# Local attention in a fused kernel: P times V on four tiles behind the scores, and two engines' order within a slot

## The reference, cut to the local attention

```python
def local_attention(q, k, v):                 # b, h, n, d = 8, 16, 256, 64
    nw = n // w                               # w = 32
    bk2, bv2 = (look(bk), look(bv))           # the previous window and the own one
    mask = (it < jb) | (it > jb + w) | (jb == -1)
    sim = jnp.einsum('bhwie,bhwje->bhwij', bq, bk2) * QK_SCALE
    sim = jnp.where(mask, -jnp.finfo(sim.dtype).max, sim)
    attn = jax.nn.softmax(sim, -1)
    out = jnp.einsum('bhwij,bhwje->bhwie', attn, bv2)

def attn_layer(x, Wqkv, qs, ksc, Wo):
    ...
    q = l2norm(q) * qs
    k = l2norm(k) * ksc
    ...
    q = q * cos * scale + rotate_half(q) * sin * scale
    k = k * cos * inv + rotate_half(k) * sin * inv
    out = local_attention(q, k, v)
    return out.transpose(0, 2, 1, 3).reshape(b, n, INNER) @ Wo
```

## Time and profile before

| | kernel before |
|---|---|
| median of three runs | 2608.39 us (2608.14 to 2609.6) |
| profiled execution | 2614.84 us |
| its span, first to last instruction | 2613.1 us |
| TensorE matmul, busy | 2374.6 us (91%) |
| VectorE, busy | 1954.8 us (75%) |
| ScalarE, busy | 1797.4 us (69%) |
| GpSimd, busy | 1083.0 us (41%) |
| mean granted TensorE clock | 0.971 of full speed |

### The profile page before, as it was taken

How to read it: one execution, slowest core, us unless ns; L and a number is a source line. 1 busy time by engine, 2 the same in 40 slices (tenths; PEclk the granted TensorE clock), 3 DMA queues, 4 the chain that set the end, 5 groups by cost and what they waited for, 6 DMA issues and landing times. The chain is left out here.

```text
span 2613.1 us, 62460 instructions
## 1 busy us (share of the span) xinstructions
PE 2374.6 (91%) x24940; PEld 1232.9 (47%) x24940; DVE 1954.8 (75%) x2595; ACT 1797.4 (69%) x2593; POOL 1083.0 (41%) x461
## 2 busy tenths in 40 slices
PE   7799999999999999999999999999999887777778
PEld 3355555455554555545545555454555432222345
DVE  5678777788777887787778787787777668999442
ACT  4677777787677776777767777677777566545533
POOL 0354444444444444444444444444444204556030
PEclk8899999999999999999999999999999988989889
DMA  0100000000000000000000000000000010000001
GB/s 21 54 2 2 2 26 10 10 2 2 15 22 11 2 2 15 22 11 2 2 14 14 19 2 2 15 14 19 2 2 2 1 37 1 0 0 0 18 25 40
DMA packets 16047, 29.92 MB, mean 11 GB/s; under 512 B 3616, under 2 KB 6064, under 8 KB 15664
## 3 DMA queue, kind: packets, MB, share of 16 engines
q1 hardware_dynamic: 15760, 25.78, 3.2%
HBM read 24.73 MB, written 1.05 MB: 10 GB/s over the span
## 5 line engine op out<-in xcount | busy, mean ns | idle before, releaser
L709 POOL TENSOR_TENSOR f_rot<-f_raw,f_tabc 128x1024 f32<-128x1024 f32 x192 | 452.9, 2359 | 682.6 <-DVE f_qk L757 299.3
L713 POOL TENSOR_TENSOR f_rot<-f_rot,f_shuf 128x1024 f32<-128x1024 f32 x192 | 453.6, 2362 | 465.1 <-DVE f_shuf L750 465.1
L607 ACT ACTIVATE f_raw<-f_ps 128x1024 f32<-128x1024 f32 x192 | 196.7, 1024 | 303.4 <-PE f_ps L431 301.6
L478 PEld LDWEIGHTS f_ps<-f_ptz,f_v 64*64 64x64 f32 x6144 | 260.1, 133 | 93.9 <-issue 93.9
L478 PE MATMUL f_ps<-f_ptz,f_v 64*64 64x96 f32 (+1 forms) x6144 | 286.4, 243 | 1.5 <-ACT f_ptz L628 1.4
L776 DVE TENSOR_REDUCE f_sum<-f_ps 128x8 f32<-128x512 f32 x192 | 131.9, 687 | 178.9 <-ACT f_ps L663 176.1
L747 DVE STREAM_SHUFFLE f_shuf<-f_raw 128x1024 f32<-128x1024 f32 x192 | 255.7, 1332 | 0.0
L757 DVE SCALAR_TENSOR_TENSOR f_qk<-f_rn,f_rot 128x1024 f32<-128x1024 f32 x192 | 233.7, 1217 | 28.9 <-POOL f_rot L713 28.9
L430 PE MATMUL f_ps<-f_xs,f_wq 128*128 128x512 f32 x384 | 216.1, 645 | 34.3 <-DVE f_xs L728 24.2
L750 DVE TENSOR_TENSOR f_shuf<-f_shuf,f_tabs 128x1024 f32<-128x1024 f32 x192 | 236.8, 1233 | 7.6
L616 ACT ACTIVATE f_rn<-f_ps 128x1024 f32<-128x1024 f32 x192 | 199.0, 1036 | 38.9 <-PE f_ps L437 38.6
(11 more groups left out here) (267 smaller groups left out, 4010.0 us busy)
## 6 DMA issues: line engine op xcount, KB each, us to landing
e_w<-in_e_w SPq DMA_DIRECT2D x16, 256.0 KB, 2.8
f_wq<-in_f_wq SPq DMA_DIRECT2D x12, 256.0 KB, 2.9
f_wk<-in_f_wk SPq DMA_DIRECT2D x12, 256.0 KB, 3.6
f_wv<-in_f_wv SPq DMA_DIRECT2D x12, 256.0 KB, 3.3
f_wo<-in_f_wo SPq DMA_DIRECT2D x6, 512.0 KB, 3.2
f_w<-in_f_w SPq DMA_DIRECT2D x6, 341.0 KB, 2.9
s_dx<-in_k_pick SPq DMA_DIRECT2D x1, 1536.0 KB, 9.4
f_w<-in_f_w SPq DMA_DIRECT2D x6, 192.0 KB, 3.4
```

The lines of the kernel that those rows point to most:

```text
L478: mm = pe.matmul(view(ps, 7 * CH + 64 * p, [1, n], p0=64 * h, rows=64), v[64 * h:64 * h + 64, p * CH + 64 * j:p * CH + 64 * j + 64], ptz[6 ...
L709: pool.tensor_tensor(view(rot, 0, [S, 4], [1, S]), view(raw, 0, [S, 4], [1, S]), view(tab_c, 0, [S, 2], [0, 2], [1, S]), ALU.mult).then_in ...
L713: pool.tensor_tensor(rot[:, :], rot[:, :], shuf[:, :], ALU.add).then_inc(sem["rot"], 1)
```

## The change

It has four parts.

- Values are laid out anew: partitions 0 to 63 hold tokens of the first sequence and 64 to 127 those of the second, for all heads, where before they held the two heads of each pair. Two matmuls of 512 columns on two tiles take the place of four of 256.
- P times V: `mix` runs its 16 matmuls of 64 rows by 64 columns on all four quarters of the array (rows by sequence, columns by head) and writes banks 6 and 7, one for each sequence. Before, they ran on two quarters and wrote bank 7. Scores, mask, exponential, `s` and the output copy are laid out to match. Since bank 6 is also that of the transposes, `turn` now waits for the output copy.
- The order on TensorE and ScalarE: `mix` stands behind the scores and ahead of the projections in every slot; the output copy stands ahead of the raw copy and the squares.
- The order on VectorE: `rotate` stands ahead of `soft_b`.

ScalarE's squares stood ahead of the exponential before as well.

```diff
--- before.py
+++ after.py
@@ -412,12 +412,10 @@
                     need(pe, sem["ln2"], i)
                 if q == 0:
                     need(pe, sem["gelu"], i * 3 - 6 + 1 + G0)
-                for r in range(2):
-                    for h in range(2):
-                        at = 128 * (q % 4) + 64 * r
-                        mm = pe.matmul(view(ps, 2 * CH + 256 * r, [1, 256], p0=64 * h, rows=64), xs[:, at:at + 64],
-                                       view(wv, CH * (q // 4) + 64 * h, [128, 4], [1, 64]),
-                                       start=(r == 0), stop=True, skip_group_check=True)
+                for b in range(2):
+                    at = S * b + 64 * (q % 4)
+                    mm = pe.matmul(view(ps, 2 * CH, [1, CH], p0=64 * b, rows=64), xs[:, at:at + 64],
+                                   wv[:, CH * (q // 4):CH * (q // 4) + CH], start=True, stop=True)
                 mm.then_inc(sem["v_mm"], 1)
 
             def project(i, j):
@@ -454,7 +452,8 @@
 
                         keys = (view(t, KOFF + WIN * w, [-WIN, 2], [1, WIN], p0=64 * h, rows=64) if w % 2 == 0
                                 else view(t, KOFF + WIN * (w - 1), [1, 2 * WIN], p0=64 * h, rows=64))
-                        mm = pe.matmul(view(ps, (4 + h) * CH + (w // 4) * 64, [1, 64], p0=WIN * (w % 4), rows=WIN),
+                        four, b = w // 4 % 2, w // 8
+                        mm = pe.matmul(view(ps, (4 + h) * CH + (2 * four + b) * 64, [1, 64], p0=WIN * (w % 4), rows=WIN),
                                        t[64 * h:64 * h + 64, WIN * w:WIN * w + WIN], keys, start=False, stop=True,
                                        skip_group_check=True)
                 mm.then_inc(sem["s_mm"], 1)
@@ -462,6 +461,7 @@
             def turn(i, j):
                 need(pe, sem["p"], i * 8 + j + 1)
                 need(pe, sem["ptz"], i * 8 + j)
+                need(pe, sem["o"], i * 8 + j)
                 for t in range(4):
                     mm = pe.transpose(view(ps, 6 * CH + 128 * t, [1, 128]), s[j % 2][:, 128 * t:128 * t + 128], ident[:, :])
                 mm.then_inc(sem["t_mm"], 1)
@@ -472,13 +472,14 @@
                 gather(sem["o"], i * 8 + j)
                 if j % 4 == 0:
                     gather(sem["v"], i * 8 + j + 4)
-                for p in range(8):
-                    n = 96 if p < 7 else 64
+                for p in range(4):
+                    n = 96 if p < 3 else 64
                     for h in range(2):
-                        mm = pe.matmul(view(ps, 7 * CH + 64 * p, [1, n], p0=64 * h, rows=64),
-                                       v[64 * h:64 * h + 64, p * CH + 64 * j:p * CH + 64 * j + 64],
-                                       ptz[64 * h:64 * h + 64, 96 * p:96 * p + n],
-                                       start=(p == 0), stop=(p == 7), skip_group_check=True)
+                        for b in range(2):
+                            mm = pe.matmul(view(ps, (6 + b) * CH + S * b + 64 * p, [1, n], p0=64 * h, rows=64),
+                                           v[64 * b:64 * b + 64, p * INNER + 128 * j + 64 * h:p * INNER + 128 * j + 64 * h + 64],
+                                           ptz[64 * b:64 * b + 64, 96 * (4 * h + p):96 * (4 * h + p) + n],
+                                           start=(p == 0), stop=(p == 3), skip_group_check=True)
                 mm.then_inc(sem["pv_mm"], 1)
 
 
@@ -533,22 +534,20 @@
                 had2, u2, b2 = (run, i, j - 2) if j >= 2 else (before, k, j + 6)
                 if run:
                     scores(i, j)
+                if had2:
+                    mix(u2, b2)
                 if before and j == 2:
                     wo_part(k, 6, 8)
                 if before and j == 6:
                     need(pe, sem["ln"], i * 8 + 8 if run else 0)
                     gate_mm(k, 1)
                     gate_mm(k, 2)
-                if j == 6 and had2:
-                    mix(u2, b2)
                 if has:
                     if j == 7:
                         values(u, a)
                     project(u, a)
                     if j != 7:
                         values(u, a)
-                if j != 6 and had2:
-                    mix(u2, b2)
                 if before and j < 2:
                     wo_part(k, 3 * j, 3 * j + 3)
                 if before and j == 3:
@@ -596,8 +595,7 @@
                 need(act, sem["v_mm"], i * 8 + q + 1)
                 if q % 4 == 0:
                     need(act, sem["pv_mm"], i * 8 - 4 + q)
-                act.activation(view(v, 2 * (q % 4) * CH + 256 * (q // 4), [CH, 2], [1, 256]),
-                               view(ps, 2 * CH, [256, 2], [1, 256]), ACT.Copy).then_inc(sem["v"], 1)
+                act.activation(view(v, INNER * (q % 4) + CH * (q // 4), [1, CH]), bank(2), ACT.Copy).then_inc(sem["v"], 1)
 
             def raw_copy(i, j):
 
@@ -632,7 +630,8 @@
                 need(act, sem["pv_mm"], i * 8 + j + 1)
                 if j == 0:
                     need(act, sem["wo_mm"], i)
-                act.activation(o[:, UNIT * j:UNIT * j + UNIT], bank(7), ACT.Copy).then_inc(sem["o"], 1)
+                act.activation(view(o, UNIT * j, [S, 2], [1, S]), view(ps, 6 * CH, [CH + S, 2], [1, S]),
+                               ACT.Copy).then_inc(sem["o"], 1)
 
             def gelu(i, f):
                 n = FB[f][1]
@@ -651,6 +650,8 @@
                     gelu(k, 1)
                     gelu(k, 2)
                     nc.scalar.preload_act_table_set(ACT_SET)
+                if had2:
+                    out_copy(u2, b2)
                 if has:
                     raw_copy(u, a)
                 if before and j == 4:
@@ -660,15 +661,13 @@
                     value_copy(u, a)
                 if run:
                     need(act, sem["shift"], i * 8 + j + 1)
-                    act.activation(view(ps, 4 * CH, [CH, 2], [64, 4], [1, 64]), view(s[j % 2], 0, [64, 2], [128, 4], [1, 64]),
+                    act.activation(view(ps, 4 * CH, [CH, 2], [1, S]), view(s[j % 2], 0, [S, 2], [1, S]),
                                    ACT.Exp, scale=8.0).then_inc(sem["exp"], 1)
                 if has and j != 5:
                     value_copy(u, a)
                 if before and j == 5:
                     need(act, sem["scaled"], k + 1)
                     act.activation(xn[:, :], xn[:, :], ACT.Identity, scale=fcol[:, 0:1], bias=fcol[:, 1:2]).then_inc(sem["xn"], 1)
-                if had2:
-                    out_copy(u2, b2)
                 if had1:
                     spread(u1, b1)
                 if has:
@@ -766,7 +765,7 @@
                                   ALU.max).then_inc(sem["max"], 1)
                 need(dve, sem["max"], i * 8 + j + 1)
                 need(dve, sem["t_mm"], i * 8 + j - 1)
-                dve.tensor_tensor(view(t, 0, [64, 2], [128, 4], [1, 64]), view(ps, 4 * CH, [CH, 2], [64, 4], [1, 64]),
+                dve.tensor_tensor(view(t, 0, [S, 2], [64, 4], [1, 64]), view(ps, 4 * CH, [CH, 2], [64, 4], [1, 64]),
                                   view(mx, 0, [4, 2], [1, 4], [0, 64]), ALU.subtract).then_inc(sem["shift"], 1)
 
             def soft_b(i, j):
@@ -807,10 +806,10 @@
                     tables(i + 1)
                 if before and j == 6:
                     hidden(k, 1)
+                if has:
+                    rotate(u, a)
                 if run:
                     soft_b(i, j)
-                if has:
-                    rotate(u, a)
                 if before and j == 2:
                     need(dve, sem["wo_mm"], k + 1)
                     dve.tensor_tensor(ycol, ycol, bank(3), ALU.add).then_inc(sem["y1"], 1)
@@ -1580,7 +1579,7 @@
     own = (c < WIN) == even
     seen = np.where(own, c % WIN <= i, c % WIN >= i)
     first = seen & (own | (np.arange(128)[:, None] >= WIN))
-    k["k_mask"] = np.concatenate([np.where(z, f(0), f(NEG)) for z in (first, seen, first, seen)], 1)
+    k["k_mask"] = np.concatenate([np.where(z, f(0), f(NEG)) for z in (first, first, seen, seen)], 1)
     k["k_ones2"] = np.full((C, C), 1.0 / DN, f)
 
     pick = np.tile(np.eye(2 * DS, dtype=f)[:, :, None], (3, 1, C)).reshape(6 * DS, 2 * DS * C)
```

## The result

The changed kernel takes 2842.74 us, the median of four runs (2838.93 to 2844.27), against 2608.99 us for the kernel before (2608.14 to 2610.78, four runs beside it). The ratio is 1.089, with a 95% interval of 1.0877 to 1.0903: slower by 234 us. The prediction was 2874, with a range of 2750 to 3000 and 0.96 on slower. The profiled execution took 2838.93 us, for a span of 2837.1.

The account below looks back on a forecast made before the run. TensorE's queue set most slots; the loop over VectorE to the next scores would take over. 9.20 us more a unit gave 221 us, plus 45 for the clock on 2614.84: 2881, as a median 2874; range 2750 to 3000.

Parts of the forecast that it names:

- The term that decides: VectorE's rotation ahead of the sums: 3.53 us from raw copy to rotation's end, on the way to TensorE's next scores.
- The slots: Attention slots of a unit: five at 10.27 us, slot 2 12.09, slot 6 14.09, slot 7 13.37; sum 90.90 against 81.70.
- The mix: P times V on TensorE: four tiles bring it from 1.41 to 0.76 us, saving 0.65 us a slot.
- the rival of the slow mix: Four tiles gain nothing for P times V: 0.65 us more in each slot's loop, 2999 us; chance 0.10.
- The step of the mix's place: P times V ahead of the projections on TensorE: its 0.76 us, formerly beside the squares, come onto the loop.
- No collision: Rival: VectorE's sine multiply gets in before GpSimd's product, 0.72 us less where it counts, 2762 us; chance 0.08.
- The clock: TensorE's clock at half speed behind stalls: one in four of 120 taken at 1.5 us, 45 us in all.
- The other side: Rival: the rotation fits into VectorE's idle time ahead of the sums, TensorE stays the bound, 2483 us; chance 0.03.

Follow-up runs that it names:

- kernel 2: The kernel before with only `rotate` moved ahead of `soft_b` on VectorE, P times V left on two tiles behind the projections: 2807.96 us, ratio 1.073.
- kernel 9: The version with four tiles, sums first and early exponential in slots 0 to 2, with only `rotate` moved ahead of `soft_b`: 2748.6 us, ratio 1.0533.
- kernel 1: The changed kernel with the rotation put back behind the sums (`soft_b`) on VectorE, all else kept: 2606.39 us, ratio 0.9964 to the kernel before.
- kernel 4: The changed kernel with P times V back behind projections and values (except slot 6) and the output copy behind the squares; rotation still first: 2735.23 us, ratio 1.0458.
- kernel 3: The changed kernel with one more wait, holding GpSimd's cosine product until VectorE's sine multiply is done: 2780.18 us, ratio 1.0638 to the kernel before.
- kernel 5: The changed kernel with unread 512-column matmuls added where TensorE idles at the end of slots 2, 3, 4, 6 and 7: 2796.38 us, ratio 1.073.
- kernel 6: The changed kernel with P times V behind projections and values (except slot 6), sums first, and slot 2's output projection behind P times V: 2594.46 us, ratio 0.9949.
- kernel 7: Four tiles, sums first, mix between projections and values, output copy between raw copy and squares, exponential ahead of raw copy in slots 0 to 2: 2515.97 us, ratio 0.9645.
- Kernel 8: The kernel before with only the exponential moved ahead of the raw copy on ScalarE in slots 0 to 2: 2596.59 us, ratio 0.9943.

## Why the prediction was right, and where it was off

**The term that decides** held. In after's slot 4 the terms are 1.12 to the mix, 0.77 mix, 2.02 to the raw copy, 1.02 raw copy, 3.53 from its end to the end of the rotation (1249.24 - 1245.71), then the sums 0.08 ahead of that end, 1.64 to the end of the multiply, and 0.15: 10.17 us, against 10.27 forecast. The 3.53 read off the first unit of the kernel before came out to the hundredth, the 1.08 us behind GpSimd's end too. That the order is the cause, and not only goes with it, is shown from both sides: it alone gives the loss (kernels 2 and 9), and its reversal alone takes it away (kernel 1).

**The slots.** Forecast and median in after: ordinary 10.27 and 10.18 to 10.22; slots 0 and 1 together 20.54 and 20.64; slot 2 12.09 and 12.05; slot 6 14.09 and 14.05; slot 7 13.37 and 13.12. In slot 6 the projections came at 1266.06 - 1261.18 = 4.88, where I had taken 4.7 between 3.8 and 5.23. The sum of a unit is 90.46 against 90.90.

**The mix.** 0.77 us, where I took 0.76 between bounds of 0.39 and 1.41; the rival of the slow mix fell. The value came from halving, and the argument for it was that four tiles write two banks; that the banks are the reason was not tried. With entering the mix takes 0.77 us for its 32 records, and 18 of the 31 distances between the starts of its records are 6 to 10 ns (mix of slot 4, after). The 0.95 us up to which the forecast's spread lets the mix go no run shows.

**The step of the mix's place** held: I said that its 0.76 us come onto the loop, and taking it off gives 0.73 and 0.80 us in slots 3 and 4 (kernel 4).

**No collision.** That rival fell with the 1.92 us. The step from "no collision" to its 2762 us was also too good: kernel 3 did away with this collision and landed at 2780, since GpSimd's products then lay beside other instructions of VectorE: the shifted copies (L728, 1318 ns in the mean against 289) and a multiply (L828, 1.4 us against 0.7). I had treated the collision as a price of one instruction; the runs show it on these as well.

**The clock** gave about the right sum from two terms that were each off, which is luck. Its 3.41 us at half speed are in the earlier trace rows: 0.50 behind a stall of 1.97 us, and 1.00 behind one of 2.13. I took 30 falls at 1.5 us, 45 us; the trace has 21, and kernel 5 prices them at 1.95 us a unit, some 46 us, or 2.2 us a fall. The forecast had one in four of five stalls a unit. In after 20 of the 21 falls come during or just behind the stalls that end slots 2 and 6 (2.1 and 3.0 us, ten each), and none behind the stall of 2.1 us that ends slot 3: the length of the stall alone doesn't decide. Why slot 7 is hit so often in kernels 2, 4 and 9 and less in after is open.

**The other side** had its deciding point: the rotation would have had to end before the exponential. In slot 4 of after the exponential ends at 1247.81, the rotation at 1249.24, 1.4 us too late, as forecast.

**What was off by 31 us** (2874 against 2842.74) is a term that I left out. I priced the new unit against a unit of 81.70 us, which is one without a turn of the program's loop. The mean of before is 82.98 us, since TensorE stands about 2 us at a turn, in the middle of the scores, and the clock falls behind it in part of the turns (to 0.50 seven times in before). I kept these as if after had them too. The scores' group of before and of after:

```profile
L457 PE MATMUL f_ps<-f_qk 64*32 64x64 f32 x12288 | 167.8, 225 | 19.5 <-issue 19.5
```

```profile
L456 PE MATMUL f_ps<-f_qk 64*32 64x64 f32 x12288 | 168.8, 229 | 0.0
```

The 19.5 us are gone. So 24 x (82.98 - 81.70) = 31 us of the time before were not there to be added to. Against the profiled executions, in which both were measured, the forecast, 2881, is 42 us too high: these 31, and 24 x 0.44 = 11 of the slots; that the medians leave just 31 is chance. The table says the same in another way: the mean unit lies 1.82 us above the sum of the slots' medians in before and in after alike, so the clock's 45 us took the place of the stalls at the turn and did not come on top of them. What took the stall away is only half settled. A wait ahead of it is enough: kernel 2, with the old instructions and the new wait, has 0.8 us left of the 19.5. But kernels 1, 6 and 7 don't show it either, and they hardly wait there; what they share is that they have 768 matmul records fewer. Kernel 8, old instructions and no wait, keeps it (units that begin a turn last 82.8 us in the mean, the others 80.8). Which property of the shorter program does it was not tried.

## What to carry to other kernels

Before moving a long step ahead of a short one on an in-order engine, write down the loop that the short one closes, with every stage of it, and ask what the long step itself waits for: here the rotation waited for this slot's raw copy, so the sums that were ready early inherited the latest input of the slot. A unit that is priced from the trace must be the mean one, with its loop turn, or the stalls that the change will hide are counted twice. And two bounds that lie close together have to be moved together: earlier exponentials alone gave 15 us, four tiles in an order that left VectorE's loop as long 9 and 13, and both with the right order 91.

## What the runs showed that I had not expected

- Work that nobody reads made the kernel faster: nine more matmuls of 512 columns a unit in idle places took 46 us off after, by holding TensorE's granted clock at 1.00 in the attention, against 0.98. In the five kernels with the rotation in front and no such matmuls it fell to 0.50 19 to 32 times, mostly at stalls of 2 to 3 us.
- A single-input `TENSOR_SCALAR` of VectorE on 64x255 suffers far more from GpSimd's product than the multiply with two inputs: 0.28 to 2.35 us, against 1.23 to 1.92. It happened to 44 of 88 in kernel 3 and to 22 in the kernel before, and to none in after.
- The stall of about 2 us at the turn of the program's loop can disappear without being touched.
- One swap of two calls, with the same instructions, is worth 233 us of 2516 (9%), more than twice the 91 us by which the best kernel beats the kernel before.
